# Expert-conditioned tokens with a routed feed-forward: bias on TensorE, picks moved between the first shared group's steps, and the last groups' conditioning rows gathered by GpSimd

## The reference, cut to what matters

```
w = weights[subjects]; b = bias[subjects]                  # (128,32,32), (128,32)
c = einsum('bct,bcd->bdt', x, w) + b[:, :, None]           # conditioned tokens
scores = softmax(c @ gate_w.T); top 2 of 8 experts         # dense_w
y = sum over chosen e of dense_w[e] * (silu(c @ w1[e].T) * (c @ w3[e].T)) @ w2[e].T
z = (silu(c @ sw1.T) * (c @ sw3.T)) @ sw2.T                # shared expert, inner size 352
x = x + y + z
```

## Time and profile before

| | |
|---|---|
| time, 3 runs | 434.66 us median (434.63 to 435.29) |
| the profiled execution | 433.91 us |
| its span, first to last instruction | 432.1 us |
| busy: TensorE, VectorE, ScalarE, GpSimd | 412.3, 308.4, 249.5, 194.9 us |
| mean granted TensorE clock | 0.984 |
| moved by DMA | 50.46 MB |

### The profile page before, as it was taken

How to read it: one execution, slowest core, us unless ns; L and a number is a source line. 1 busy time by engine, 2 the same in 40 slices (tenths; PEclk the granted TensorE clock), 3 DMA queues, 4 the chain that set the end, 5 groups by cost and what they waited for, 6 DMA issues and landing times.

```text
span 432.1 us, 8635 instructions
## 1 busy us (share of the span) xinstructions
PE 412.3 (95%) x2931; PEld 332.9 (77%) x2931; DVE 308.4 (71%) x728; ACT 249.5 (58%) x551; POOL 194.9 (45%) x198
## 2 busy tenths in 40 slices
PE   5998599999999999999999999999999999999995
PEld 4665488887789999999999997885765756657553
DVE  6974977898786676666666664759686786776844
ACT  2888426668235656655566554347475484664754
POOL 2035009930454455444554403656575675755020
PEclk9799699999999999999999999999999999999999
DMA  8997120000036565555655622221142232322111
GB/s 243 377 383 279 58 60 0 2 0 2 25 87 201 161 173 163 156 160 162 179 159 156 155 89 89 83 85 50 50 134 86 74 109 72 114 85 62 49 51 49
DMA packets 37258, 50.46 MB, mean 117 GB/s; under 512 B 4480, under 2 KB 30464, under 8 KB 37216
## 3 DMA queue, kind: packets, MB, share of 16 engines
q1 hardware_dynamic: 29600, 31.53, 21.6%
q0 software_dynamic: 6480, 17.70, 15.5%
q10 hardware_dynamic: 1136, 0.66, 0.7%
HBM read 32.19 MB, written 17.69 MB: 115 GB/s over the span
## 4 chain that ended last, share of the span: by engine, by line
PE 87%; ACT 5%; DVE 4%; DMA 1%; issue 1%; POOL 0%; DVEq 0%; ACTq 0%
PE bank L1127 18%; PE bank L1129 17%; PE bank L1128 17%; PE bank L1395 14%; PE bank L1410 6%; PE bank L1281 4%; PE bank L1320 2%; PE bank L1319 2%; PE bank L1301 2%; PE bank L1361 2%; ACT xtr L469 2%; PE bank L1150 1%; PE bank L1140 1%; PE bank L1208 1%; PE bank L1302 1%
## 5 line engine op out<-in xcount | busy, mean ns | idle before, releaser
L404 POOL DMA_INDIRECT xg<-kept,perm x71 | 68.7, 967 | 89.8 <-PE bank L1281 55.4
L1395 PE MATMUL bank<-h,wg 128*128 128x512 fp8e4 x256 | 61.6, 380 | 0.2 <-issue 0.2
L1127 PE MATMUL bank<-w13h,xgl 128*128 x142 | 48.8, 343 | 0.0
L1395 PEld LDWEIGHTS bank<-h,wg 128*128 128x128 fp8e4 x256 | 22.1, 97 | 33.9 <-ACT ff L638 12.1
L411 POOL DMA_INDIRECT ga<-slots_out,slot x32 | 32.8, 1026 | 33.3 <-SPq L347 17.3
L958 DVE TENSOR_TENSOR hrl<-bank,hrh 128x256 fp32r<-128x256 f32 (+1 forms) x36 | 15.2, 421 | 44.1 <-issue 35.6
L1129 PE MATMUL bank<-w13h,xgh 128*128 x142 | 45.5, 320 | 0.0
L1128 PE MATMUL bank<-w13l,xgh 128*128 x142 | 45.5, 320 | 0.0
L636 ACT ACTIVATE gel<-bank 128x512 bf16<-128x512 f32 x64 | 40.1, 627 | 6.4 <-PE bank L1395 3.3
L411 POOL DMA_INDIRECT gb<-slots_out,slot x32 | 37.7, 1179 | 9.8 <-issue 9.8
L638 ACT ACTIVATE ff<-bank 128x512 bf16<-128x512 f32 x64 | 40.6, 634 | 0.0
(11 more groups left out here) (196 smaller groups left out, 1168.4 us busy)
## 6 DMA issues: line engine op xcount, KB each, us to landing
slots_out<-yr SPq DMA_DIRECT2D x35, 256.0 KB
xres<-in_x SPq DMA_DIRECT2D x7, 512.0 KB, 10.9
kept<-xtr SPq DMA_DIRECT2D x7, 512.0 KB, 6.8
out_x<-fin SPq DMA_DIRECT2D x7, 512.0 KB
w13raw<-in_rw SPq DMA_DIRECT2D x8, 352.0 KB, 4.2
w2raw<-in_rw SPq DMA_DIRECT2D x8, 256.0 KB, 5.4
wgst<-in_wgate SPq DMA_DIRECT2D x16, 128.0 KB
xg<-kept,perm POOLq DMA_INDIRECT x71
```

The source lines that it names most:

```text
L404: pool.indirect_dma_start(out=xg[:, i % 2, j, :], out_offset=None, in_=kept, in_offset=bass.IndirectOffsetOnAxis(perm[:, 2 * i + j:2 * i + ...
L1127: pe.matmul(dst, al, bh, start=first, stop=False, skip_group_check=True)
L1395: ins = pe.matmul(bank[bk][:, :], wg8[:, kk, half, c * P:(c + 1) * P], h8[:, k, kk, :], start=(kk == 0), stop=(kk == KC - 1))
```

## The change: what it does

- The biases come from four small matmuls on TensorE: the bias table times a one-hot of the subjects on 8 partitions (`hot_out`), made by VectorE from a new small input `pick`, which GpSimd loads. ScalarE copies the result from PSUM to `bias`. The GpSimd product and the VectorE reduction go.
- VectorE selects rows for groups 0 to 5 only. For groups 6 and 7 it computes row indices (`rowi`), and GpSimd gathers the rows of the 8 tiles from DRAM by indirect DMA, in four pairs, each behind the selection of another group.
- TensorE's 40 warm-up matmuls become 22 before the bias matmuls, 22 after them and 11 after the first conditioning.
- The shared weights are loaded ahead of x groups 5 to 7.
- The two halves of the logits get a bank each (4 and 5), so the second half waits for nothing of the first.
- In group 0 VectorE's picks are spread between `hidden_mul`, `hidden_lo` and `shared_x_lo(1)`; ScalarE's silu, rounding of x, of h and of the experts' weights, and the exponential of the softmax are put in another order; TensorE starts with the last transposes and waits for the shared down weights only before `shared_down`.

```diff
-WARM = 40
+WARM = 22
+SELECTED = GROUPS - 2
...
-            for g in range(1, GROUPS):
+            for g in range(1, 5):
                 load_x(g)
             sp.dma_start(swst[:, :], sw13).then_inc(s("sw_in"), 16)
             sp.dma_start(sw2st[:, :], sw2).then_inc(s("sw_in"), 16)
+            for g in range(5, GROUPS):
+                load_x(g)
...
             pool.memset(onesb[:, :], 1.0).then_inc(s("c_prep"), 1)
+            pool.dma_start(pick[:, :], pick_in).then_inc(s("pick_in"), 16)
...
-            pool.tensor_tensor(bias_of[:, :, :], hot[:, TILES:, :], tabr[:, CH:TROW, :].broadcast_to([P, TILES, E]), ALU.mult
-                               ).then_inc(s("bias_made"), 1)
             pool.memset(gate4[:, :, :, :], 0.0).then_inc(s("gate_spread"), 1)
+
+            def gather_rows(n):
+                pool.wait_ge(s("rows_ready"), n + 1)
+                for k in (2 * n, 2 * n + 1):
+                    t = SELECTED * GT + k
+                    pool.indirect_dma_start(out=wrow[:, t, :], out_offset=None, in_=weights,
+                                            in_offset=bass.IndirectOffsetOnAxis(rowi[:, k:k + 1], 0)).then_inc(w_in[t // GT], 16)
+
+            pool.wait_ge(s("rowi_ready"), 1)
+            gather_rows(0)
+            gather_rows(1)
             pool.wait_ge(s("gate_in"), 32)
...
+            gather_rows(2)
+            gather_rows(3)
             pool.wait_ge(s("sw_in"), 32)
...
+            act.wait_ge(s("bias_made"), 1)
+            act.activation(bias[:, :], bank[5][:, 0:TILES], ACT.Copy).then_inc(s("bias_ready"), 1)
             conditioned(0)
             for g in range(1, GROUPS):
                 conditioned(g)
-                if g == HALF + 2:
+                keep_xT(g - 1)
+                if g == HALF + 1:
                     keep_raw(0)
-                keep_xT(g - 1)
             keep_xT(GROUPS - 1)
-            shared_x_hi(1)
...
+            act.wait_ge(kept_early, 16 * (GROUPS - 2))
+            shared_silu(0, 0)
+            keep_raw(1)
+            shared_x_hi(1)
+            shared_h_hi(0, 0, first=True)
+            shared_silu(0, 1)
             act.wait_ge(s("sw_split"), KC + 1)
             act.wait_ge(s("xt_ready"), TILES)
-            keep_raw(1)
             routed_weight_hi(0)
-            act.wait_ge(kept_early, 16 * (GROUPS - 2))
-            shared_silu(0, 0)
+            shared_h_hi(0, 1)
+            shared_silu(0, 2)
             routed_weight_hi(1)
-            shared_h_hi(0, 0, first=True)
+            shared_h_hi(0, 2)
             act.wait_ge(s("m_sub"), 1)
             act.activation(r2[:, :, :], r1[:, :, :], ACT.Exp).then_inc(s("m_exp"), 1)
-            shared_act(0, chunks=(1, 2))
...
+            dve.tensor_scalar(rowi[:, :], front[:, SELECTED * GT:TILES], float(CH), front[:, TILES + E:].bitcast(F32),
+                              ALU.mult, ALU.add).then_inc(s("rowi_ready"), 1)
+            dve.wait_ge(s("pick_in"), 16)
+            dve.tensor_scalar(hot_out[:, :], pick[:, 0:BATCH], pick[:, BATCH + CH:BATCH + CH + 1].bitcast(F32),
+                              pick[:, BATCH + CH + 1:].bitcast(F32), ALU.is_equal, ALU.mult).then_inc(s("out_ready"), 1)
...
             select_rows(0, GT)
-            dve.wait_ge(s("bias_made"), 1)
-            dve.tensor_reduce(bias[:, :], bias_of[:, :, :], AX.X, ALU.add).then_inc(s("bias_ready"), 1)
-            select_rows(GT, 2 * GT)
-
-            for i in range(2, GROUPS):
+            for i in range(1, SELECTED):
                 select_rows(i * GT, (i + 1) * GT)
+            shared_weight_lo(0)
+            shared_weight_lo(1)
+            shared_x_lo(0)
+            shared_weight_lo(2)
...
-            shared_weight_lo(2)
-            shared_x_lo(0)
-            shared_x_lo(1)
...
+            shifted(0)
             hidden_mul(0, 0)
+            shifted(1).then_inc(s("m_sub"), 1)
             hidden_lo(0, 0)
...
             nearest(oh1[:, :, :])
+            hidden_mul(0, 1)
             link(dve.scalar_tensor_tensor(r3[:, :, :], oh1[:, :, :], MASKED, r1[:, :, :], ALU.mult, ALU.add))
+            hidden_lo(0, 1)
+            shared_x_lo(1)
             nearest(r3[:, :, :])
+            hidden_mul(0, 2)
             link(dve.tensor_tensor(r3[:, :, :], r3[:, :, :], desc, ALU.mult))
-            hidden_mul(0, 1)
+            hidden_lo(0, 2)
             nearest(oh2[:, :, :])
-            hidden_lo(0, 1)
-            hidden_mul(0, 2)
...
-            hidden_lo(0, 2)
             shared_x_lo(2)
...
+            def ones(n):
+                for _ in range(n):
+                    pe.matmul(bank[7][:, 0:P], onesb[:, :], onesb[:, :], start=True, stop=True)
+
+            ones(WARM)
+            pe.wait_ge(s("out_ready"), 1)
+            for j in range(GT):
+                ins = pe.matmul(bank[5][j * CH:(j + 1) * CH, 0:TILES], pick[:, BATCH:BATCH + CH].bitcast(F32),
+                                hot_out[:, j * TILES:(j + 1) * TILES], start=True, stop=True, tile_position=(0, j * CH))
+            ins.then_inc(s("bias_made"), 1)
+            ones(WARM)
             condition(0)
+            ones(WARM // 2)
...
-            pe.wait_ge(s("sw_split"), KC + 1)
-            pe.wait_ge(s("xt_ready"), (GROUPS - 1) * BPT + 1)
-            shared_up(0, True, parts=[0])
             transpose_xt(GROUPS - 1)
             router(GROUPS - 2)
+            pe.wait_ge(s("sw_split"), KC)
+            shared_up(0, True, parts=[0])
+            router(GROUPS - 1)
             shared_up(0, True, parts=[1])
-            router(GROUPS - 1)
-            shared_up(0, True, parts=[2])
             logits(1)
-            shared_up(0, True, parts=range(3, 6))
+            shared_up(0, True, parts=range(2, 6))
+            pe.wait_ge(s("sw_split"), KC + 1)
             shared_down(0, first=True, chunks=range(2))
```

More of the change, by code:

```diff
@@ L66, in tiles_of, with adaln_ffn @@
     return min(2, USED_TILES - 2 * i)
-def adaln_ffn(nc, front_in, adapters, consts, table, x, gate, sw13, sw2, rw13, rw2, l1w, scal, wgate, wlin, out, kept, slots_out):
+def adaln_ffn(nc, front_in, pick_in, adapters, consts, table, weights, x, gate, sw13, sw2, rw13, rw2, l1w, scal, wgate, wlin, out, kept, slots_out):
     x_t = x.rearrange("(g j p) f -> g p j f", j=GT, p=P)
@@ L102, in adaln_ffn @@
         early = [base[0]]
-        tabr = at("tabr", [P, TROW, E], F32, early)
-        hot = at("hot", [P, 2 * TILES, E], F32, early)
+        tabr = at("tabr", [P, CH, E], F32, early)
+        hot = at("hot", [P, TILES, E], F32, early)
         wrow = at("wrow", [P, TILES, CH], F32, early)
@@ L107, in adaln_ffn @@
         early[0] = base[0] + 4 * KC * SHARED * 4
-        front = at("front", [P, 2 * TILES + E], I32, early)
+        front = at("front", [P, TILES + E + 1], I32, early)
+        rowi = at("rowi", [P, TILES - SELECTED * GT], I32, early)
+        pick = at("pick", [E, BATCH + CH + 2], I32, early)
+        hot_out = at("hot_out", [E, BATCH], F32, early)
         xtr_last = at("xtr_last", [P, GT, D], F32, early)
-        bias_of = at("bias_of", [P, TILES, E], F32, early)
         bias = at("bias", [P, TILES], F32, early)
@@ L275, in adaln_ffn @@
         x_in = [sem(f"x_in{g}") for g in range(GROUPS)]
+        w_in = [sem(f"w_in{g}") for g in range(GROUPS)]
         rw_in = [sem(f"rw_in{e}") for e in range(E)]
@@ L1131, in condition @@
             def condition(i):
-                pe.wait_ge(s("rows_ready"), i + 1)
+                if i < SELECTED:
+                    pe.wait_ge(s("rows_ready"), i + 1)
+                else:
+                    pe.wait_ge(w_in[i], GT * 16)
                 for sem_in in x_first if i == 0 else [x_in[i]]:
@@ L1169, in logits @@
                 pe.wait_ge(s("raw_kept"), h + 1)
-                pe.transpose(bank[5][:, h * P:(h + 1) * P], lraw[:, h, :], ident).then_inc(s("logit_psum"), 1)
+                pe.transpose(bank[4 + h][:, P:2 * P], lraw[:, h, :], ident).then_inc(s("logit_psum"), 1)
             pe.wait_ge(s("c_prep"), 1)
-            for _ in range(WARM):
-                pe.matmul(bank[3][:, 0:P], onesb[:, :], onesb[:, :], start=True, stop=True)
+            def ones(n):
[8 more added lines that the diff above has]
+            ones(WARM)
             condition(0)
+            ones(WARM // 2)
             pe.wait_ge(s("shapes_in"), 16)
@@ L1523 @@
         "front": np.concatenate([np.repeat(itok_B_0_7, CH).reshape(TILES, P).T,
-                                 np.repeat(subjects.transpose(0, 2, 1), CH).reshape(TILES, P).T, shapes.view(np.int32)], 1),
+                                 shapes.view(np.int32), (np.arange(P) % CH).astype(f)[:, None].view(np.int32)], 1),
+        "pick": np.concatenate([np.tile(subjects.transpose(1, 0, 2).reshape(1, BATCH), (E, 1)),
+                                np.concatenate([fside_8xS_0.reshape(E, CH), np.arange(E, dtype=f)[:, None], np.ones((E, 1), f)],
+                                               1).view(np.int32)], 1),
         "adapters": itok_B_0_6,
         "consts": _constants(),
```

(3 more changed lines are left out.)

37 lines of the change are left out of this document (14 added, 23 removed).

## The result

The changed kernel takes 436.87 us (median of 10 executions, 435.82 to 438.50), the kernel before 434.65 (10, 434.05 to 435.96): ratio 1.0052, 95% interval 1.0034 to 1.0069. I had forecast 429.5 and a gain.

A forecast was written before the change was run, and what follows sets the result against it. TensorE was taken as the bound, with 87% of the last-ending chain. Ranks 6.8 us earlier less 1.6 given back made 5.2 won: 433.91 to 428.7 profiled, 429.5 against the median; range 425.5 to 433.0.

The forecast's parts named there:

- the price of nothing: Front: four pairs of gathers take GpSimd 8.8 us, ending about 17.3, covered by ScalarE's pace, so they cost nothing.
- the signs by which I had said it would be wrong: Bias load landing past 5.5, products stretched beside gathers, or the clock falling again near 44.
- The bias load: Front: GpSimd's load of the bias picks lands at 4.2, taken as 4.3; conditioning then starts at 7.6.
- First eviction: Front: ScalarE's first eviction at 7.8 instead of 9.28, its table load now under cover; 1.5 won.
- 2.5 us per group: Front: each group takes 2.5 on VectorE and ScalarE, before 2.66; group 5 evicted from 20.3 instead of 22.56.
- Gathers and VectorE: Front: gathers hold VectorE up by 0.1 at most, so they were priced at nothing there.
- The third rival: Gathers lock VectorE: each pair holds back one product by about 0.9, 3.6 in all; near 432.8; chance 5%.
- The clock: TensorE's clock full in the front and first shared group; it was taken to fall only after 2.4 us of idleness.
- The price of a warm-up: Front: each warm-up matmul costs 0.111 us, so the 22 behind the bias matmuls end at 7.6.
- my slower rival: Bias load after 5.5: TensorE idles, clock falls, second 22 warm-ups take 4.9; 436.4 if landed at 8.0; chance 9%.
- The lock in the first shared group: First shared group: GpSimd's four expert subtractions from 36.7 alternate with VectorE, which waits 4.9 in all.
- First shared product to ranks: First shared group: first shared product at 29.5, ranks at 50.0, which is 6.8 ahead of the kernel before.

The follow-up runs named there:

- g3: The changed kernel without gathers, VectorE selecting all eight groups, and with the bias table loaded from ScalarE's queue: 430.13 us.
- h3: The changed kernel with its eight gathers back to back from the first selected rows on (about 9 us), gate copies behind them: 435.57 us.
- e2: The kernel before, with the same four pairs of gathers added into a scratch tile that nobody reads: 434.51 us.
- f3: The changed kernel without the 22 warm-ups between bias matmuls and first conditioning, the 11 later ones kept: 439.90 us.
- e3: The changed kernel with its gathers, but 40 warm-ups first as before and none later: 431.33 us.
- i2: The changed kernel with 30 warm-ups first instead of 22, the later 22 and 11 kept: 436.88 us.
- i1: The changed kernel with 40 long-met waits added at an idle place of SyncE's program and at the ends of GpSimd's and TensorE's: 436.52 us.
- f1: The changed kernel unaltered, run again for a second profile: 438.95 us, one execution.
- g1: The kernel with 40 warm-ups first and none later, gathers as in the changed kernel, run again unaltered: 430.60 us.
- h4: The changed kernel with all eight gathers run from the row numbers on and the bias table loaded from ScalarE's queue: 430.44 us.
- f2: The changed kernel without the 11 warm-ups behind the first conditioning: 438.43 us.

## Why the prediction was wrong

**The step that failed** is the price of nothing that the forecast of the front put on the gathers: "The four pairs of gathers cost GpSimd 4 x 2.2 = 8.8 ... So all of this lies under ScalarE's pace and costs nothing", and with it "I take the clock as full". I asked what a gather does to GpSimd and to VectorE, and never what it does to TensorE. The first shared product was to start at 29.5 and started at 37.98. Taking the gathers out (e1) gives 7.4 of this back, making them plain loads (e4) 7.6, halving them (g2) 6.8, starting them at 4 us (g4) 6.8. No kernel without gathers stalled (e1, e4, g3), and no kernel whose gathers were fewer or ran from 4 us. So the loss needs the gathers, and needs them there. The stall costs 8.4 us by the spans of two single executions (435.4 against e1's 427.0), and 7.5 by the medians (436.87 against 429.40), or 6.8 with each against the kernel before on its own chip.

None of the signs by which I had said it would be wrong came true: the load landed at 5.4 and not past 5.5, no product was stretched beside gathers, and the clock didn't fall near 44. TensorE beside gathers was not among them.

**What is not settled** is why TensorE slows down. It takes the gathers and, with them, warm-ups in certain places: five arrangements stall, three don't (22, 40 or 48 first and none later), and h3 has the warm-ups of the changed kernel and its gathers at nearly the same times (the first four 0.2 us later, the last four 0.5 to 1 us earlier) and doesn't. The slow step 1 of the changed kernel is over before its last four gathers start, so their earlier place alone can't have freed that step in h3. Ruled out as sufficient or as needed are the gathers alone (e2), their bytes and destination (e4), a low clock (f3), the number of instructions ahead (f3 against e3), a shift of eight places in the program (i2), 40 more instructions in three programs (i1), and an accident of one execution (f1, g1). I have no rule left that sorts all the kernels; the cause inside TensorE stays open.

The other steps, in their order:

- *The bias load.* Predicted landed at 4.3; issued at 1.30 it landed 4.1 later, at 5.4. VectorE waited 1.84 for it, which puts rows and conditioning 1.0 later than in my sum (8.58 against 7.6). The DMA issue row, and VectorE's timeline:

```profile
pick<-in_pick POOLq DMA_DIRECT2D x1, 5.1 KB, 4.1
```
```profile
3.41 0.23 DVE L712 TENSOR_SCALAR rowi<-front 128x8 int32<-128x8 int32 x1
5.47 0.33 DVE L715 TENSOR_SCALAR hot_out<-pick 8x128 f32<-8x128 int32 x1 [1.84 <-DMA pick<-in_pick]
5.73 1.21 DVE L722 TENSOR_TENSOR prod<-tabr,hot 128x1024 f32<-128x1024 f32 x1
...
10.74 1.22 DVE L722 TENSOR_TENSOR prod<-tabr,hot 128x1024 f32<-128x1024 f32 x1
```

  I had 2.0 from the end of the issue to the landing, from a late gather when the DMA share was 0.26 (115 to 119 us); here it was 3.4, at a DMA share of 1.01 (2.0 to 5.4). The Trainium skill, DMA: Bandwidth & Descriptors, Anatomy of one DMA — SWDGE (gpsimd) path, gives about 2.0 us as the fixed part for this path; beside full queues this load took 4.1 from the start of its issue, twice that.
- *First eviction.* Predicted 7.8, 0.2 behind the start of conditioning. It came 1.21 behind it (8.58, 9.79), and in e1 too (8.07, 9.28). The bank is handed over at the end of its matmuls, and the earlier trace rows had 7.24 and 7.99 in them, 0.75 apart; I overlooked it. Here the 32 matmuls also took 1.16 instead of 0.73.
- *2.5 us per group.* Right where there is no stall: e1 evicts group 2 at 13.79 and group 5 at 21.19, 2.47 each. With load and first eviction mis-sized, a clean front reaches the first shared product at 30.61 (e1) to 31.2 (g2, g4), not at 29.5: the front loses 0.5 to 1.1 against 30.11.
- *Gathers and VectorE.* Right for VectorE: products take 1.21 to 1.23 beside the gathers, as without. The third rival falls. GpSimd ended them at 20.31, where I had 17.3, and began its casts at 20.33 instead of 18.8; TensorE did not wait for the casts. The rule of the Trainium skill weighed there (SBUF — State Buffer, Who interferes with whom) does not bite for gathers in this trace.
- *The clock.* Wrong, 0.63 from 15.5 to 28. It fell within the stall, while no wait of TensorE's weight loads was over 0.6 us. The 2.4 us of idleness that I read off one hole are no rule: in i2 it was at the lower level from 7.8 on, and TensorE's longest wait before was 1.42.
- *The price of a warm-up.* Not settled. The second block of 22 took 2.53 us, 0.115 each, as I had it; in i2 the same block took 1.40, 0.064 each. Both stand at a granted clock of 1.00 (6.0 to 8.5 and 6.0 to 7.4). So doubling 0.111 for a low clock, as my slower rival did, had no row behind it.
- *The lock in the first shared group.* Right, to a few tenths. These are VectorE's timeline and GpSimd's in that stretch:

```profile
45.84 1.61 DVE L832 SCALAR_TENSOR_TENSOR r<-oh,r 128x256 f32<-128x256 f32 x1
47.49 1.67 DVE L786 TENSOR_TENSOR hsl<-hsf,hsh 118x512 fp32r<-118x512 f32 x1
49.08 2.72 DVE L735 TENSOR_TENSOR xtL<-xtT,xsh 128x1024 fp32r<-128x1024 f32 x1
...
52.16 1.07 DVE L826 TENSOR_TENSOR r<-r,s 128x256 f32<-128x256 f32 x1
...
58.21 1.20 DVE L735 TENSOR_TENSOR xtL<-xtT,xsh 128x1024 fp32r<-128x1024 f32 x1
```
```profile
45.46 1.70 POOL L401 TENSOR_TENSOR w13l<-w13raw,w13h 128x704 fp32r<-128x704 f32 x1 [21.89 <-ACT w2h L539]
47.12 1.49 POOL L401 TENSOR_TENSOR w2l<-w2raw,w2h 128x512 fp32r<-128x512 f32 x1
48.57 2.15 POOL L401 TENSOR_TENSOR w13l<-w13raw,w13h 128x704 fp32r<-128x704 f32 x1
50.68 2.27 POOL L401 TENSOR_TENSOR w2l<-w2raw,w2h 128x512 fp32r<-128x512 f32 x1
```

  Four VectorE ops are stretched, the four that I had named; xtL takes 2.72 beside GpSimd's subtractions and 1.20 without. Together they lose 4.3 us (1.2, 1.0, 1.5 and 0.7); I had 4.9, whose four terms add up to 4.8. With that rule of the Trainium skill the trace agrees for computing instructions of both engines. TensorE's waits from 39 to 59 us (total, times, longest) were to be 0.4, 1.4, 0.9 and 1.4:

```profile
PEld bank L1225 <- DVE upto L842: 1.4, 1, 1.4
PEld bank L1150 <- DVE xtL L735: 1.2, 1, 1.2
PEld bank L1150 <- DVE hsf L779: 1.0, 1, 1.0
PEld bank L1150 <- DVE hsl L786: 0.6, 2, 0.3
```

- *First shared product to ranks.* Predicted 20.5 (29.5 to 50.0), measured 20.37, with the clock at 1.00; before it was 26.67. It is 20.35 to 20.37 in all but two of the profiles with the change, stalled or not, and 20.66 and 20.67 in h4 and g3; e2, which lacks it, has 26.70.
- *Given back behind ranks.* Predicted 1.6. From ranks to the end of the span: before 375.3, e1 376.0, g4 376.9, changed 377.1, so 0.7 to 1.8; the most is 378.1 (f3).

The sum of a kernel without the stall is then -0.5 (front) + 6.3 (group) - 0.7 (given back) = 5.1, and the spans say 432.1 - 427.0 = 5.1. The medians say 4.6 (434.00 and 429.40). My 5.2 was near for that kernel by luck in part: the front was 1.1 worse than I had it, the give-back 0.9 smaller. In g4, which keeps the gathers, the terms are -1.1 + 6.3 - 1.6 = 3.6, by the spans 3.7 and by the medians 4.9. The rival that ends slower had the sign and nearly the time (436.4) but not the mechanism: its load was to land after 5.5 and the second block of 22 warm-ups to take 4.9; it landed at 5.4, they took 2.53.

## What to carry to other kernels

Price a newly placed gather against every engine that is busy beside it, TensorE first, and try it early, late and in smaller number before it is kept: here eight gathers cost about 7 us at one place and nothing measurable five microseconds earlier. When a change has two separate parts, measure each alone; one won 6.0 to 6.3 us in every kernel and the sum still came out slower. An engine that shows as busy can be stalled: count its instructions per window, not its busy time.

## What the runs showed of the hardware that I had not expected

- The same 32 conditioning matmuls took 0.7 to 1.5 us in the kernels with the change that didn't stall, and up to 5.72 in the stall (f2), in runs of a few with gaps of about 0.5 us that the profile puts down to "issue", and with the granted clock at 1.00 throughout (f3). Eight GpSimd gathers stood beside each case of it, and plain GpSimd loads of the same bytes didn't cause it (e4). But h3 and e3 have the eight gathers and run clean.
- A 5.1 KB load from GpSimd at 1.3 us took 4.1 us to land beside full queues; from ScalarE's queue it was there by 3.42.
- TensorE stopped for 1.95 us in the middle of a run of matmuls while one block of instructions came in through full queues (g3, one execution). That the one caused the other is argued, not shown.
- A 20.35 us stretch of four engines repeated to 0.02 us in sixteen profiles, so a shift of its start is passed on whole.
